# FFN of an adaLN block: half-precision parts for gate, up and down, weights split by GpSimd, last addition on ScalarE and GpSimd

## What is computed

```python
def fp4_quant_dequant(x):                      # blocks of 16 along the last dim
    scale = jnp.max(jnp.abs(xb), axis=-1, keepdims=True) / 6.0
    scale = jnp.maximum(scale, jnp.float32(1e-12))
    idx = jnp.searchsorted(_MID, jnp.abs(xb / scale))
    return _GRID[idx] * sign(xb) * scale       # 0, .5, 1, 1.5, 2, 3, 4, 6
def fp4_linear(x, w): return einsum('bsk,nk->bsn', quant(x), quant(w))
mod = (silu(c) @ wmod).reshape(2, 6, 1, -1)
sa, ca, ga, sb, cb, gb = mod[:, 0], ..., mod[:, 5]     # |ga|, |gb| >= 0.25
h = layernorm(x) * (1 + ca) + sa
x = x + ga * attention(h)                      # softmax over the queries' axis
h = layernorm(x) * (1 + cb) + sb
x = x + gb * fp4_linear(silu(fp4_linear(h, w_gate)) * fp4_linear(h, w_up), w_down)
```

## Time and profile before

| | |
|---|---|
| median of 3 runs | 1684.09 us (1681.34 to 1684.48) |
| the profiled execution | 1685.73 us |
| its span | 1684.4 us |
| TensorE busy | 1640.7 us (97%) |
| VectorE busy | 1578.9 us (94%) |
| ScalarE busy | 1374.7 us (82%) |
| GpSimd busy | 779.4 us (46%) |
| chain that ended last | VectorE 64%, TensorE 32% |

### The profile page before, as it was taken

How to read it: one execution, slowest core, us unless ns; L and a number is a source line. 1 busy time by engine, 2 the same in 40 slices (tenths; PEclk the granted TensorE clock), 3 DMA queues, 4 the chain that set the end, 5 groups by cost and what they waited for, 6 DMA issues and landing times.

```text
span 1684.4 us, 38849 instructions
## 1 busy us (share of the span) xinstructions
PE 1640.7 (97%) x15454; PEld 817.2 (49%) x15454; DVE 1578.9 (94%) x1705; ACT 1374.7 (82%) x2508; POOL 779.4 (46%) x1625
## 2 busy tenths in 40 slices
PE   9999999999999999999999999999999999999998
PEld 8743333333333333673333333333333379999997
DVE  7899999999999999769999999999999879888887
ACT  5599999999999999569999999999999833333332
POOL 3034445444444545303454544566654457555542
PEclk8999999999999999999999999999999999999999
DMA  6102111112111112511111121111112533534420
GB/s 232 65 9 72 51 49 46 45 50 67 52 51 51 46 45 76 168 38 45 46 45 45 45 70 50 52 51 46 46 45 64 157 113 126 155 125 155 145 67 19
DMA packets 83110, 123.15 MB, mean 73 GB/s; under 512 B 4713, under 2 KB 69105, under 8 KB 82929
## 3 DMA queue, kind: packets, MB, share of 16 engines
q1 hardware_dynamic: 82512, 120.15, 22.5%
q10 hardware_dynamic: 416, 0.53, 0.1%
HBM read 74.52 MB, written 46.15 MB: 72 GB/s over the span
## 4 chain that ended last, share of the span: by engine, by line
DVE 64%; PE 32%; issue 2%; ACT 1%; POOL 1%; DMA 0%; POOLq 0%; DVEq 0%
DVE nm L1073 60%; PE acc L447 13%; PE slot L447 10%; PE acc L615 6%; PE slot L671 1%; PE slot L586 1%; DVE ost L1086 1%; ACT e_sb L825 1%; PE slot L468 0%; PE acc L646 0%; DVE qs L1140 0%; DMA v_sb<-in_x 0%; DVE e_sb L1128 0%; DVE e_sb L1147 0%; PE slot L494 0%
## 5 line engine op out<-in xcount | busy, mean ns | idle before, releaser
L1073 DVE TENSOR_REDUCE nm<-slot 128x1 f32<-128x1024 f32 x1024 | 1166.1, 1213 | 20.2 <-PE slot L586 18.0
L825 ACT ACTIVATE e_sb<-slot,nm 128x1024 f32<-128x1024 f32 x1024 | 1137.6, 1113 | 17.5 <-DVE nm L1073 12.5
L615 PE MATMUL acc<-e_sb,vp 64*64 64x512 f32 x8192 | 1060.7, 594 | 6.3 <-DVE ost L1086 4.7
L586 PE MATMUL slot<-stq,stk 64*64 64x512 f16 x4096 | 411.6, 388 | 21.6 <-ACT e_sb L825 21.6
L586 PEld LDWEIGHTS slot<-stq,stk 64*64 64x64 f16 x4096 | 117.6, 103 | 626.5 <-ACT e_sb L825 592.7
L615 PEld LDWEIGHTS acc<-e_sb,vp 64*64 64x64 f32 x8192 | 283.3, 132 | 188.1 <-issue 73.8
L1309 POOL TENSOR_TENSOR dlt<-nm 128x4 f32<-128x4 f32 x128 | 25.8, 202 | 408.2 <-DVE nm L1073 408.2
L825 ACT ACTIVATION_READ_ACCUMULATOR e_sb<-slot,nm 128x1 f32 x1024 | 199.8, 195 | 0.0
L1300 POOL TENSOR_TENSOR vp<-v_sb,fac 128x512 f32<-128x512 f32 x128 | 133.6, 1044 | 10.2 <-POOL fac L1290 0.3
L1286 POOL TENSOR_TENSOR rtot<-tot,mone 128x4 f32<-128x4 f32 x128 | 132.8, 1038 | 10.0
L1280 POOL TENSOR_TENSOR wsum<-cor,ssum 128x8 f32<-128x8 f32 x128 | 26.0, 203 | 233.7 <-ACT cor L855 233.7
(11 more groups left out here) (180 smaller groups left out, 1931.5 us busy)
## 6 DMA issues: line engine op xcount, KB each, us to landing
o_r<-o_heads SPq DMA_DIRECT2D x32, 1024.0 KB, 7.2
stk<-qk_parts SPq DMA_DIRECT2D x128, 128.0 KB
o_heads<-ost_hi SPq DMA_DIRECT2D x64, 256.0 KB, 3.4
o_heads<-ost SPq DMA_DIRECT2D x64, 256.0 KB, 4.1
v_sb<-in_x SPq DMA_DIRECT2D x16, 512.0 KB, 6.1
qk_parts<-e_sb SPq DMA_DIRECT2D x32, 256.0 KB, 2.3
stq<-qk_parts SPq DMA_DIRECT2D x128, 64.0 KB
out<-e_sb SPq DMA_DIRECT2D x32, 128.0 KB, 1.8
```

Source lines behind the costliest of these rows:

```text
L586: mm = pe.matmul(slot[s][side * VD:(side + 1) * VD, c * 512:(c + 1) * 512], stk[c * 64:c * 64 + 64, h % 2, i * P + side * VD:i * P + (side ...
L615: mm = pe.matmul(acc[half * VD:(half + 1) * VD, c * 512:(c + 1) * 512], vp[rows, g % 3, gi, half, :], e_v[rows, j % ERING, n0:n0 + 512], s ...
L825: act.activation(e_v[:, j % ERING, half * 1024:(half + 1) * 1024], slot[u % 3][:, :], ACT.Exp, bias=nm[:, g % 4, i, half:half + 1], accum_ ...
L1073: dve.tensor_reduce(nm[:, g % 4, i, half:half + 1], slot[u % 3][:, :], AX.X, ALU.max, negate=True).then_inc(maxed.sem)
```

## The change

The operands of gate, up and down become half precision (F16), high and low part as before. So that they fit into its range, all of them are levelled, that is multiplied by powers of two: the weights and inputs by factors found once (`levels`), the hidden values by one per token (`h_lift`), and ScalarE, VectorE and GpSimd multiply the factors out again (`undo_gu`, `h_undo`). For the factors the largest quantised weight of each matrix goes through two small transfers to all partitions (`tops_d`). The weights are split by GpSimd alone, in the attention of the second batch (`split_gate_up`, eight pieces of three instructions; `fold_wd(0, c)`), and for the second batch's down weights in every other step from 4 to 14 of the last stage. The last addition of a tile becomes a scaled copy on ScalarE (`take_down`) and an addition on GpSimd (`add_out`); only the last tile's stays on VectorE. The scales of a tile have a buffer for even and odd steps (`grid`), and `mix_snap(i)` stands ahead of `token_moments(i + 1)`.

The diff, cut:

```diff
+        wgu_hi = [place(f"wgu_hi{k}", [P, 2 * F], at, F16) for k, at in enumerate(wgu_at)]
+        wgu_lo = [place(f"wgu_lo{k}", [P, 2 * F], at + 2816, F16) for k, at in enumerate(wgu_at)]
+        xqT_hi = place("xqT_hi", [P, 2, 2 * P], WQ_AT, F16)
...
@@ def down
-                pe.wait_ge(*out_made.past(i - 1))
+                pe.wait_ge(*down_taken.past(i - 1))
@@ def take_values_act
+            if b and i == 2:
+                act.wait_ge(*top_made.past(1))
+                act.dma_start(tops_d[1].unsqueeze(1), tops[:, 2:3]).then_inc(tops_out.sem, 16)
+            if b and i == 4:
+                act.wait_ge(*tops_read.past(0))
+                act.wait_ge(*tops_out.past(1))
+                act.dma_start(all_tops[:, :], tops_d[1:2].to_broadcast([P, P])).then_inc(got_tops.sem, 16)
@@ def attend_act
-                    act.wait_ge(*vp_made.past(B * JG - 1))
-                    for k in range(2):
-                        high(wgu_hi[k][:, :], wguT[:, k, :]).then_inc(wgu_high.sem)
+                    act.wait_ge(*levels_made.past(0))
@@
-            high(xqT_hi[:, i % 2].rearrange("p a b -> p (a b)"), acc[:, 768:1024]).then_inc(xq_high.sem)
+            act.activation(xqT_hi[:, i % 2, :], acc[:, 768:1024], ACT.Copy, scale=lift[:, 1 + b:2 + b]).then_inc(xq_high.sem)
+
+        def take_down(i):
+            act.wait_ge(*down_mm.past(i))
+            act.wait_ge(*xq_low.past(min(i + 3, TILES - 1)))
+            if i >= 3:
+                act.wait_ge(*out_out[i % 3].past(i // 3 - 1))
+            act.activation(outb[:, i % 3, :], down_at(i), ACT.Copy,
+                           scale=h_undo[:, (i + 3) % 4:(i + 3) % 4 + 1]).then_inc(down_taken.sem)
@@ def scalar_program
+                if i >= 5:
+                    take_down(i - 5)
                 if i <= TILES + 1:
                     silu(i - 2)
-                if i == 2:
-                    split_down_act(0)
-                if i == NT:
-                    split_down_act(1)
@@ def attend_dve
-                        low(dve, wgu_lo[:, i, :], wguT[:, i, :], wgu_hi[i][:, :]).then_inc(wgu_low.sem)
@@ def mix_normalise
+            if lo == 0:
+                dve.tensor_reduce(h_top[:, i % 4:i % 4 + 1], grid[:, i % 2, 0:44], AX.X, ALU.max)
+            settle(dve.reciprocal(inv, scale))
+            if lo == 0:
+                top = h_top[:, i % 4:i % 4 + 1].bitcast(I32)
+                dve.tensor_scalar(h_lift[:, i % 4:i % 4 + 1].bitcast(I32), top, EXPONENT, EXPONENT,
+                                  ALU.bitwise_xor, ALU.bitwise_and)
+                dve.tensor_scalar(h_size[:, i % 4:i % 4 + 1].bitcast(I32), top, EXPONENT, None, ALU.bitwise_and)
@@ def mix_snap
             dve.wait_ge(*mix_added.past(i - 1))
+            if lo == 0:
+                dve.tensor_scalar(grid[:, i % 2, 0:44], grid[:, i % 2, 0:44], h_lift[:, i % 4:i % 4 + 1], 2.0 ** 11, ALU.mult, ALU.mult)
@@ def vector_program
-                if i >= 5:
+                if i - 5 == TILES - 1:
                     finish(i - 5)
+                if i <= TILES + 2:
+                    mix_snap(i)
                 if i + 1 < TILES:
                     token_moments(i + 1)
-                if i <= TILES + 2:
-                    mix_snap(i)
-                if i == 3:
-                    split_down_dve(0)
-                if i == NT:
-                    split_down_dve(1)
@@ def split_gate_up, new
+            pool.tensor_scalar(wguT[:, k, cols], wguT[:, k, cols], lift[:, 0:1], None, ALU.mult).then_inc(sem)
+            pool.tensor_copy(wgu_hi[k][:, cols], wguT[:, k, cols]).then_inc(sem)
+            pool.tensor_tensor(wgu_lo[k][:, cols], wguT[:, k, cols], wgu_hi[k][:, cols], ALU.subtract).then_inc(gu_split.sem)
@@ def fold_wd
-            pool.tensor_tensor(wdb[b][:, c, :], wdT[:, c, :], gb[:, b, :], ALU.mult).then_inc(wd_folded.sem)
+            pool.tensor_tensor(wd_fold[:, :], wdT[:, c, :], gb[:, b, :], ALU.mult).then_inc(sem)
+            pool.tensor_copy(wdb_hi[b][:, c, :], wd_fold[:, :]).then_inc(sem)
+            pool.tensor_tensor(wdb_lo[b][c], wd_fold[:, :], wdb_hi[b][:, c, :], ALU.subtract).then_inc(wd_split.sem)
@@ new
+        def add_out(i):
+            pool.wait_ge(*down_taken.past(i))
+            pool.tensor_tensor(outb[:, i % 3, :], outb[:, i % 3, :], x2_r[:, i % 7, :], ALU.add).then_inc(out_made.sem)
@@ def gpsimd_program
+                if i >= 5:
+                    add_out(i - 5)
                 scale_mix(i)
                 if i + 1 < TILES:
                     inverse_root2(i + 1)
-                if 4 <= i < 4 + FCH:
-                    fold_wd(1, i - 4)
+                if 4 <= i < 4 + 2 * FCH and i % 2 == 0:
+                    fold_wd(1, (i - 4) // 2)
```

More of the change, by code:

```diff
@@ L153, in adaln_block @@
         qs = sb("qs", [P, 3, 88])
+        tops = sb("tops", [P, 2 * B])
+        all_tops = sb("all_tops", [P, P])
+        peak = sb("peak", [P, 5])
+        size = sb("size", [P, 5])
+        lift = sb("lift", [P, 5])
+        undo = sb("undo", [P, 5])
+        undo_gu = sb("undo_gu", [P, B])
+        wide_max = sb("wide_max", [P, 4, B])
+        h_top = sb("h_top", [P, 4])
+        h_lift = sb("h_lift", [P, 4])
+        h_size = sb("h_size", [P, 4])
+        h_undo = sb("h_undo", [P, 4])
         constants = sb("constants", [P, 2])
@@ L1049, in prepare_dve @@
             step = 0
+            if b:
+                dve.wait_ge(*got_tops.past(0))
+                dve.tensor_reduce(peak[:, 0:1], all_tops[:, :], AX.X, ALU.max).then_inc(tops_read.sem)
             for g in range(NG):
```

157 lines of the change are left out of this document (107 added, 50 removed).

## The result

| | before | after |
|---|---|---|
| median, us | 1684.43 (20 runs, 1681.34 to 1687.43) | 1687.12 (20 runs, 1683.29 to 1690.99) |
| ratio | | 1.0015, 95% interval 1.0008 to 1.0022 |
| profiled execution, us | 1685.73 (span 1684.4) | 1689.26 (span 1688.0) |

The time that was forecast, 1672, did not come; the result lies just outside the range, above it, and above the kernel before.

A forecast was written before the change was run, and what follows sets the result against it. TensorE bounds the last stage, VectorE 0.9 us a tile behind. Period 9.77 to 9.38 over 25 tiles (-9.8), down weights -2.3, start -2.2, folds +2.5: -11.8 us, giving 1672 as median; range 1665 to 1686.

The forecast's parts named there:

- (6): Splits on GpSimd: 0 in the attention; last-stage folds, some 1.9 us for three instructions, cost +2.5 us, ends 0 and 6.
- (7): Levels in batch 2's preparation: ScalarE's wait and VectorE's small instructions stay hidden, 0; with that cover gone, up to 3 us.
- (8): End: loops of the last four tiles lose 0.3 us on matmuls and gain 0.5 in small instructions; 0.
- (1): Last-stage gate, up and down matmuls: half precision saves 0.47 us a tile, TensorE's sum becomes 9.30.
- Rival C: Half-precision matmuls have the same gap, TensorE stays at 9.77 us a tile; -4.3 us, 1680, chance 0.12.
- (5): Down-weight splits leave ScalarE and VectorE: -2.3 us at the second batch's split, -2.2 at the start of the last stage.
- (2): VectorE in a last-stage tile: last addition leaves (0.41 us), four small instructions come (0.5), making 8.94 us.
- (4): Last addition on ScalarE and GpSimd: GpSimd's 0.74 us addition costs VectorE's second snap about 0.3; VectorE 9.24, period 9.38.
- rival D: GpSimd between the snaps delays both engines: period 10.05, 1691.5 us, chance 0.12; against it, busy GpSimd tiles still averaged 9.77.

The follow-up runs named there:

- e6_read_later: Changed kernel with ScalarE issuing the read of the tops back to every partition at step 6 instead of step 4 of batch 2's preparation; 1684.09 us.
- e3: Changed kernel with the same 19 GpSimd fold instructions laid out over 17 steps, one to a step (two at two steps); 1683.00 us.

## Why the prediction was wrong

The steady tile came as forecast; three other terms did not. In the profiled executions the result is 15.4 us above the forecast. Term (6) is 5.8 of that, term (7) with what else lies ahead of tile 0 another 5.8, term (8) 4.5, and the start of the loop gave back 0.7.

- **(1) half precision**: right. 0.46 us a tile, forecast 0.47: the starts lie 0.150 and 0.109 us apart, 3 ns above the columns at 2.4 GHz. By the Trainium skill (TensorE: Matmul & The Clock Gate, Back-to-back issue gap) it would be about 2.5 ns, a figure that the page gives for a matmul by itself; the trace agrees. Rival C is out (the two terms of (5) give its price as -4.5, not -4.3).
- **(2) and (4) the period**: right in sum, 9.38 (steps of 9.31 to 9.39 from tile 16 to 29), and 5.2 us saved in those 13 tiles. Where the clash sits was read a little wrong: not the second snap loses 0.3, but the small scaling 0.34 and the first snap 0.10. What I did not ask is what the addition's own place buys: 0.41 leaves VectorE, 0.44 comes back as standing, and GpSimd has 1.52 us more of its time taken, not 0.74. "The 0.41 that leaves is sure" was false.
- **(5) down weights and start**: right. The 2.3 at tile 15 are gone, and tile 0 to 3 saved 2.87, forecast 2.2. Half of that may be the clock and not the splits: 1.44 of it lie in the step from tile 2 to 3, where the kernel before has a stretch at the lower level and no profile of the changed kernel has one (1.00 in 1364 to 1384). The forecast had left open whether it stays.
- **(6) folds, mis-sized**: forecast +2.5 with ends 0 and 6. Over 13 steps of 9.38, tiles 3 to 16 took 8.5 more. My 1.9 us for a fold's three instructions were 0.74 twice and a copy, durations of instructions that meet nobody. Here they are 1.28, 0.40 and 1.71 (3.4 us, and 0.94 for the scaling ahead of the first), and the addition is 1.52, so GpSimd had a full tile's work and more (no idle time from 1393.80 on), which my "against" in rival D denied. The measured cost of the folds is 6.3 in lumps. The split of the last head had a price (about 2) as soon as the tile was shorter than what it needs.
- **(7) levels, the step that failed outright**: forecast 0. I allowed "even at 5 us each" for two tiny transfers, and asked of them only whether VectorE would be done in time. For ScalarE I counted its first wait, for the top of the weights (4.05 us, and hidden as forecast), and not the second, for the landing of the write that it must see before it issues the read. The write took 8.47, ScalarE stands 6.49 with its copies behind it, and that uses up TensorE's free quarters. "With that cover gone, up to 3" is near the standing alone (3), and left out the clock: +5.0 in the profiled execution, and 2.5 to 3 in the median by e6_read_later.
- **(8) end, forecast 0**: +4.5 in the profiled execution. I counted instructions and no clock. Shorter products with a chain on VectorE that is no shorter mean longer gaps on TensorE (2.28 against 1.48). About 1.4 of the 4.5 stay where the clock is 1.00 (17.6 against 17.2 for tile 29 to 31 in e3, 22.2 against 21.1 behind it in e6), and about 3 are the two lower stretches of this execution. In all profiles each fall from tile 29 on starts in a gap of 1.5 to 2.9 us or within 1.3 us behind one, but not each such gap brings a fall.

Of the rivals, D named GpSimd as the engine that eats the gain, and the fold tiles are of its kind, but its price (a period of 10.05 throughout) did not come.

## What to carry to other kernels

Before moving an instruction to an idle engine, ask what it will stand beside: on these two engines its price is its own time plus the standing, and the engine it leaves may stand for it as long as it had worked (0.44 us for 0.41 here). Work that is placed in another's idle time has to fit in the room of each single step, so lay it out one instruction at a time. When an engine has to wait for a transfer between two issues, price that wait by what is queued behind it, and put the second issue where the landing is surely past. Before crediting an edit with 2 us, see in the trace whether they lie where the edit is.
